# A hybrid network of convolution, scan, attention and experts: its first stage rebuilt

## The reference

```python
out = relu(group_norm(conv(x, w1)))                 # 256 -> 64 channels
om = conv(out, w_off, pad=1) + b_off                # 27 maps: 9 x, 9 y, 9 masks
mask = sigmoid(om[:, 18:])
py, px = grid_y + ky + om[:, 9:18], grid_x + kx + om[:, :9]
sampled = bilinear_sample(out, py, px) * mask       # 9 taps a pixel
out = einsum('bckhw,ock->bohw', sampled, w2)
out = relu(group_norm(out))
x1 = relu(group_norm(conv(out, w3)) + x)            # 64 -> 256 channels
h = group_norm(x1)
# pixel order of each of two heads, from four numbers a, b, c, d
w = (a * z + b) / (c * z + d + 1e-6)                # z: complex point of a pixel
perm = argsort(real(w) + 1.3 * imag(w))
```

## Time and profile before

| | |
|---|---|
| time of the whole program, median of 3 runs | 942.29 us (939.59 to 943.25) |
| profiled execution, first to last instruction (span) | 936.3 us |
| TensorE busy | 764.8 us, 82% of the span |
| VectorE busy | 594.6 us, 64% |
| ScalarE busy | 483.4 us, 52% |
| POOL busy | 298.5 us, 32% |

### The profile page before, as it was taken

How to read it: one execution, slowest core, us unless ns; L and a number is a source line. 1 busy time by engine, 2 the same in 40 slices (tenths; PEclk the granted TensorE clock), 3 DMA queues, 4 the chain that set the end, 5 groups by cost and what they waited for, 6 DMA issues and landing times. The chain is left out here.

```text
span 936.3 us, 17800 instructions
## 1 busy us (share of the span) xinstructions
PE 764.8 (82%) x6400; PEld 431.4 (46%) x6400; DVE 594.6 (64%) x1303; ACT 483.4 (52%) x618; POOL 298.5 (32%) x246
## 2 busy tenths in 40 slices
PE   3959638999988798649999667787659999999993
PEld 1848426633664465533444244454534444444442
DVE  4985343399777674466667376564576777677763
ACT  4134134643134556237778324445337877778871
POOL 1061000077220100034555220334024444566640
PEclk8579857999989999769999979889879999999996
DMA  3000036000023430431111243792523156522114
GB/s 119 1 0 1 0 121 295 1 0 1 1 66 100 131 94 4 140 112 35 46 47 41 67 128 99 229 250 79 174 84 105 49 184 239 187 69 70 64 57 147
DMA packets 55197, 85.21 MB, mean 91 GB/s; under 512 B 10532, under 2 KB 46500, under 8 KB 51908
## 3 DMA queue, kind: packets, MB, share of 16 engines
q1 hardware_dynamic: 48040, 67.42, 22.5%
q0 software_dynamic: 7072, 16.66, 5.4%
HBM read 59.01 MB, written 12.32 MB: 76 GB/s over the span
## 5 line engine op out<-in xcount | busy, mean ns | idle before, releaser
L2162 PE MATMUL psum<-ring,f_x_t 128*32 x432 | 197.1, 599 | 2.4 <-DVE f_x_t L1970 2.4
L2166 PE MATMUL psum<-f_w_up,f_x_t 128*32 128x512 f32 x864 | 197.4, 599 | 0.0
L1976 DVE COPY f_w_up<-ring 128x2048 f32 x108 | 131.5, 1219 | 12.8 <-issue 12.1
L2064 ACT ACTIVATE f_w_down<-ring 128x1024 f32 x108 | 108.2, 1056 | 0.0
L2187 PE MATMUL psum<-ring,f_gated_t 128*32 x432 | 102.1, 379 | 1.7 <-issue 1.7
L2191 PE MATMUL psum<-f_w_down,f_gated_t 128*32 128x256 f32 x1296 | 102.8, 379 | 0.0
L2166 PE MATMUL psum<-h,f_x_t 128*32 128x512 f32 x216 | 99.3, 603 | 0.0
L2166 PE MATMUL psum<-x,f_x_t 128*32 128x512 f32 x216 | 97.8, 595 | 0.0
L2162 PEld LDWEIGHTS psum<-ring,f_x_t 128*32 128x32 f32 x432 | 43.3, 110 | 109.9 <-issue 109.9
L1859 POOL DMA_INDIRECT rows_out<-f_y,f_to_row x36 | 64.6, 1795 | 89.6 <-DVE f_y L1992 51.2
L1850 POOL DMA_INDIRECT f_xs<-rows_in,f_from_row x54 | 74.8, 1386 | 40.1 <-PE psum L2150 20.7
(11 more groups left out here) (298 smaller groups left out, 1674.9 us busy)
## 6 DMA issues: line engine op xcount, KB each, us to landing
ring<-in_f_experts SPq DMA_DIRECT2D x24, 1536.0 KB, 7.6
a_stack_q<-a_parts SPq DMA_DIRECT2D x96, 64.0 KB, 2.0
a_stack_k<-a_parts SPq DMA_DIRECT2D x96, 64.0 KB, 2.0
rows_in<-h SPq DMA_DIRECT2D x4, 1024.0 KB, 12.1
ring<-rows_out SPq DMA_DIRECT2D x8, 512.0 KB, 5.5
earlier_y<-f_y POOLq DMA_DIRECT2D x18, 128.0 KB, 2.9
f_earlier_y<-earlier_y POOLq DMA_DIRECT2D x18, 128.0 KB, 3.2
ring<-in_a_wqkv SPq DMA_DIRECT2D x2, 768.0 KB, 4.4
```

The source lines that it names most:

```text
L1976: dve.tensor_copy(w_up[tile, q % 2], k.ring[:, bass.ds(at[tile - 1], 2 * CT * CHUNK)]).then_inc(s_uv, 1)
L2064: act.activation(w_down[:, tile - 1, q % 2, :], k.ring[:, bass.ds(at[tile - 2] + 2 * CT * CHUNK, CHUNK // P * C)], ACT.Copy).then_inc(s_da, 1)
L2162: pe.matmul(psum[0:QUARTER, 2 * b + side, :], x_t[:, b, t, 0:QUARTER], k.ring[:, bass.ds(at + start, CHUNK)], start=first, stop=final, til ...
L2166: last = pe.matmul(psum[rows, 2 * b + side, :], x_t[:, b, t, rows], w_up[tile, b][:, start:start + CHUNK], start=first, stop=final, tile_p ...
```

## The change

All of it is in the first stage and in the arrays prepared for it.

- Loads: x in two halves, each with a semaphore; the identity, the norm's tensors and w_off under semaphores of their own. ScalarE's queue loads `mobius` and `z`; `z` holds only a partition's own two pixels. TensorE starts with three products on w1.
- Scores: `scores` computes only the partition's own two pixels for both heads, 25 steps of up to 8 elements, ahead of the first statistics. `spread` turns them on TensorE, so that every partition has all 256 in PSUM. `rank` is eight VectorE steps and a reduction, behind the image; POOL makes the one-hot rows.
- Image: one padded image on all 128 partitions, without shifted copies: two images by ScalarE, two by VectorE in two steps each. POOL makes an unpadded copy, `plain`.
- Offsets: w_off is the stationary operand, 32 columns on tiles of 64 rows x 32 columns; the lower 64 partitions have taps 0 to 4, the upper ones taps 5 to 8, in two banks, and one column tile belongs to one image. ScalarE and VectorE add the two, TensorE turns the sum.
- Weights: six pieces of two images and three taps; all outer products on VectorE, four of 768 elements a piece, all evictions of turns on ScalarE. `mix` runs as two 64-row halves; VectorE takes four of the eight.
- Sampling: 18 steps, each with the turns of one tap of two images, then the sampling of the tap before.
- Tail: statistics straight from PSUM, eight and four identity products around the second group mean, the second norm's result by ScalarE and VectorE, the third convolution on 64-row halves, image pair by image pair.

The core of the diff:

```diff
@@ PixelOrder
+    def spread(self, pe, bank, ident):
+        pe.wait_ge(self.s_value, 1)
+        for h in range(HEADS):
+            for t in range(NT):
+                last = pe.transpose(bank[:, N * h + P * t:N * h + P * t + P],
+                                    self.value[:, h, t:t + 1].broadcast_to([P, P]), ident)
+        last.then_inc(self.s_spread, 1)
...
+                dve.scalar_tensor_tensor(self.tie[:, NT * h + t, :], scores, self.value[:, h, t:t + 1], self.before[:, t, :],
                                          ALU.is_equal, ALU.mult).then_inc(self.s_rank, 1)
...
+                dve.scalar_tensor_tensor(self.less[:, i, :], scores, self.value[:, h, t:t + 1], self.tie[:, i, :],
+                                         ALU.is_lt, ALU.add).then_inc(self.s_rank, 1)
...
+        dve.tensor_reduce(self.rank_of[:].rearrange("p h t -> p (h t)"), self.less[:], AX_X, ALU.add).then_inc(self.s_rank, 1)
@@ gpsimd
-                pool.tensor_tensor(weights[:, b % 2, 1, :, :].rearrange("p k (y x) -> p k y x", y=HW),
...
+            pool.wait_ge(s_img, B)
             for b in range(B):
+                pool.tensor_copy(plain[:, b].rearrange("p (y x) -> p y x", y=HW),
+                                 image[:, b, 1:HW + 1, 1:HW + 1]).then_inc(s_plain, 1)
+            order.one_hot(pool)
@@ vector
+            order.scores(dve)
...
+            for i, b in enumerate((2, 3)):
+                inner = image[:, b, 1:HW + 1, 1:HW + 1]
+                dve.tensor_scalar(inner, psum[:, y_banks + 1, N * i:N * i + N].rearrange("p (y x) -> p y x", y=HW),
+                                  g1.scale[:, b:b + 1], g1.shift[:, b:b + 1], ALU.mult, ALU.add).then_inc(s_scaled, 1)
+                dve.wait_ge(s_scaled, i + 1)
+                dve.tensor_scalar(inner, inner, 0.0, None, ALU.max).then_inc(s_img, 1)
+            order.rank(dve, psum[:, SCORE_BANK, :])
...
+            def sampling(q):
+                dve.wait_ge(s_hat, q + 1)
+                if q >= 2:
+                    dve.wait_ge(s_tr, PAIR_LOADS * (q - 1))
+                for half in range(2):
+                    for t in range(NT):
+                        T = NT * half + t
+                        dve.tensor_tensor(weights[:, q % 2, half, t].rearrange("p k (y x) -> p k y x", y=HW),
+                                          hat[:, q, T, KT:, :].unsqueeze(3).broadcast_to([P, KT, HW, HW]),
+                                          hat[:, q, T, :KT, :].unsqueeze(2).broadcast_to([P, KT, HW, HW]),
+                                          ALU.mult).then_inc(s_wd, 1)
...
+            distances(0)
+            distances(1)
+            take_mixed(1)
             mask_hats(0)
             sampling(0)
+            distances(2)
             mask_hats(1)
+            sampling(1)
+            take_mixed(4)
+            distances(3)
+            mask_hats(2)
+            sampling(2)
+            take_mixed(5)
...
@@ scalar
+            for q in range(PIECES):
+                for j in range(PAIR_LOADS):
+                    J = PAIR_LOADS * q + j
+                    b, tap = 2 * (q // THIRDS) + j % 2, KT * (q % THIRDS) + j // 2
+                    act.wait_ge(s_tr, J + 1)
+                    act.activation(weights_t[:, b, tap].rearrange("p s n -> p (s n)"), psum[:, J % 4, :], ACT.Copy).then_inc(s_ev, 1)
+                    if j == 1 and q + 2 < PIECES:
+                        tents(q + 2)
+                    if q == 2 and j == PAIR_LOADS - 1:
+                        take_mixed(7)
@@ tensor
+            for n in range(FIRST_TAPS):
+                for j in range(B):
+                    pe_rows = slice(QUARTER * j, QUARTER * j + QUARTER)
+                    for channels, tap, bank in ((lower, n, OM_BANKS[0]), (upper, FIRST_TAPS + n, OM_BANKS[1])):
+                        if tap >= TAPS:
+                            continue
+                        final = tap in (FIRST_TAPS - 1, TAPS - 1)
+                        last = pe.matmul(psum[pe_rows, bank, 0:N], w_off[channels, n, :],
+                                         image[channels, j, tap // 3:tap // 3 + HW, tap % 3:tap % 3 + HW],
+                                         start=(n == 0), stop=final,
+                                         tile_position=(channels.start, QUARTER * j))
...
+            for u in range(PIECES * KT):
+                for half in range(2):
+                    turn(u // KT, 2 * (u % KT) + half)
+                if u:
+                    sample(u - 1)
+                if u in MIX_AFTER:
+                    i = MIX_AFTER[u]
+                    if i == 4:
+                        pe.wait_ge(s_moa, 2)
+                    else:
+                        pe.wait_ge(s_mod, i - 3)
+                    mix(i)
+            sample(PIECES * KT - 1)
+            square_identity(pe, k, psum[:, SPARE_BANK, :], 4)
+            g2.group_mean(pe, psum[:, 4, 0:2 * PAIRS], pair[:])
+            square_identity(pe, k, psum[:, SPARE_BANK, :], 8)
```

More of the change, by code:

```diff
@@ L189, in products @@
[L189 to L213, removed]
@@ L447, in _ @@
         def _(act):
+            order.load_points(act, k)
             order.root(act)
@@ L476, in _ @@
[L476 to L484 removed]
+            take_mixed(0)
@@ L506, in _ @@
             pe.wait_ge(s_w1, 16)
-            pe.wait_ge(s_x, 16)
+            for _ in range(3):
+                pe.matmul(psum[:, SPARE_BANK, 0:P], w1[:, 0, :], w1[:, 0, :], start=True, stop=True)
             for half in range(2):
+                pe.wait_ge(s_x[half], 16)
                 for t in range(CT):
@@ L549, in sample @@
+            def sample(u):
+                i, tap = u // TAPS, u % TAPS
+                if u == 0:
+                    pe.wait_ge(s_moa, 3)
+                    pe.wait_ge(s_mod, 1)
+                if u == TAPS:
+                    pe.wait_ge(s_moa, 4)
+                    pe.wait_ge(s_mod, 4)
+                pe.wait_ge(s_ev, 2 * (u + 1))
+                for s in range(NT):
                     for half in range(2):
@@ L575, in _ @@
-            sample(1)
-            g2.group_mean(pe, psum[:, 4, 0:B], pair[:])
-            pe.wait_ge(s_r2, B // 2)
-            for t in range(CT):
-                for b in range(B):
-                    last = pe.matmul(psum[:, 2 * t + b // 2, (b % 2) * N:(b % 2) * N + N], w3[:, b % 2, P * t:P * t + P],
-                                     r2[:, b // 2, :], start=True, stop=True)
-                    if b % 2:
-                        last.then_inc(s_c3, 1)
+                                         mixed[:, b, s, tap, :], weights_t[:, b, tap, s, :],
@@ new lines, in sample @@
+                                         start=(tap == 0 and s == 0), stop=(tap == TAPS - 1 and s == NT - 1))
+                if tap == TAPS - 1:
+                    last.then_inc(s_y, 1)
+            pe.wait_ge(s_w, LOADED)
+            mix(0)
+            pe.wait_ge(s_omc, 1)
+            turned = psum[:, OM_T_BANK, 0:TT * QUARTER].rearrange("p (b s o) -> p b s o", b=B, s=NT)
+            for s in range(NT):
+                last = pe.transpose(turned[:, :, s, :], om_c[:, P * s:P * s + P], k.ident_sb[:])
@@ new lines, in _ @@
+            last.then_inc(s_omt, 1)
+            mix(1)
+            pe.wait_ge(s_moa, 1)
+            mix(2)
+            pe.wait_ge(s_mod, 1)
+            mix(3)
+            pe.wait_ge(order.s_rank, order.READ)
+            pe.wait_ge(s_mask, 1)
+            for u in range(PIECES * KT):
+                for half in range(2):
+                    turn(u // KT, 2 * (u % KT) + half)
[8 more added lines that the diff above has]
+                    mix(i)
```

498 lines of the change are left out of this document (259 added, 239 removed).

## The result

Four runs of the changed kernel have a median of 901.14 us (898.85 to 906.88), four of the kernel before, beside them, 942.77 (939.59 to 943.69): ratio 0.9561, 95% interval 0.9515 to 0.9607. The forecast was 903, between 890 and 921. The profiled execution took 901.77 us, its span is 900.0.

The account below looks back on a forecast made before the run. The limit changes by stretch (DMA, norm chain, TensorE, outer products, serial tail). First stage 67.1 + 8.1 + 15.6 = 90.8 against 129.7, 38.9 less; 936.3 - 38.9 = 897.4, plus 6.0 gives 903 us, range 890 to 921.

Parts of the forecast that it names:

- row halves do not overlap: Rival: offsets' row halves run one after another, taking 15.5 us, mixes 1.0 more; 915 us in all; chance 0.10.
- VectorE paces the loop: Rival: a three-tap product costs 2.0 us, 24 take 48, loop ends near 79; 916 us in all; chance 0.06.
- TensorE stays at its lower level: Rival: TensorE at 1.2 GHz through the stage, loop 77.2 us for 38.6; 948, up to 970; low clock chance 0.06.
- The change gives little: Rival: front and tail already paced by DMA and omitted chains; 921 us in all; chance 0.04.
- part 5: Loop of turns, sampling and mixes, 49.2 us before: 18 steps of 1.97, mixes 3.5, 39.0 in all; last sample at 67.1.
- Part 1: Loads and scores, up to 15.95 us before: 2.5 us earlier, bounds 0 and 4; norm ready at 13.5.
- Part 2: Image, 5.85 us before: ScalarE and VectorE write side by side, shifted copies go; 1.4 us, ready at 14.9.
- Part 3: Offsets, 20.68 us before: 72 records in 3.9 us, VectorE's ranks 5.1 end last at 20.0; positions at 21.3.
- Part 4: Positions to first turn: distance steps, eviction, mask and four products take 5.4 us; first image pair complete at 26.7.
- The clock's charge of 1.8: Loop start: 4 us of work at half pace, as TensorE pauses ahead of the loop; 1.8 us net.
- Part 6: Tail, last sample to last statistic: 8.1 us against 11.7, or 11 with the clock low; the 15.6 behind stays.
- The 6.0 us that I added: Whole kernel: median of shown runs lies 6.0 us above the profiled span, added to the predicted span of 897.4.

Follow-up runs that it names:

- sixth experiment: Changed kernel with the offset product running all taps of the lower 64 rows first, then all of the upper; 905.06 us, 0.962 of the kernel before.
- eleventh experiment: Changed kernel with six warming products, groups of three taps, later ranks' reduction and six identity squares ahead of mix 3; 895.31 us, 0.9491 of the kernel before.
- fifth experiment: Changed kernel with sampling in groups of three taps, one piece behind the turns, and the last mix one step later; 900.44 us, 0.9556 of the kernel before.
- tenth experiment: Changed kernel with nine identity products added in TensorE's pauses between offsets and loop; 902.87 us, 0.955 of the kernel before.
- third: Changed kernel with all nine taps of two images turned first, then nine samplings in one block; 909.21 us, 0.9634 of the kernel before.
- seventh experiment: Changed kernel without the eight and four identity products around the second group mean; 906.43 us, 0.9609 of the kernel before.

## Why the prediction was right, and which terms were off

Each step of the sum, from the end of the one ahead of it, in us:

```
step                                predicted  measured  difference
loads and norm, to the image           13.5      16.2      +2.7
image                                   1.4       1.8      +0.4
image to positions                      6.4       5.4      -1.0
positions to first pair's products      5.4       6.0      +0.6
products to last sample                40.4      41.4      +1.0
last sample to last statistic           8.1       7.9      -0.2
to stage two                           15.6      15.7      +0.1
stage two at                           90.8      94.4      +3.6
```

**The mechanism held.** The image, the offsets, the loop and the tail shrank where the prediction put it, and TensorE became the bound of the loop, as its 41.37 busy of 41.40 us show. Against *row halves do not overlap*: 72 records in 2.39 us, where one after another they were put at 15.5. My 3.9 (four at once) was too high: eight start within 0.05 us of each other, and such groups follow 0.215 apart. A mix has its turns start 0.69 behind its own start (36.54 to 37.23), nearer to the overlapped end than my 0.9. Against *VectorE paces the loop*: 24 products have a mean of 0.958 us, and VectorE is busy 23.52 of 41.40. Against *TensorE stays at its lower level*: the granted clock is 1.00 from 36 us on. *The change gives little* was priced at 921, and the time is 901. One of the prediction's own signs of being wrong did appear, a granted clock of 0.50 past 32 us: it lasted until about 35 and is priced under part 5.

**Part 1 failed.** I took 2.5 us off the norm; nothing came off (16.16 here, 15.98 in the earlier trace rows). x in halves starts the convolution 0.4 earlier (5.96 for 6.35), but its eight records take 6.34 us, 5.25 before: most of the first six start 0.85 apart, and from 11.2 us on they follow at about half of that. The granted-clock column reads 1.00 throughout this stretch, but the trace's entries on the clock begin only at 11.31, and in all 13 profiles the first entry (7.56 to 11.85 us) stands in the record in which the pace doubles; before it the column shows no measurement. That ties the pace to the granted clock. What stands ahead of the convolution moves that rise, but does not settle it: with six products and no pause the eight records take 4.52 to 5.26 us (three profiles), with three and a pause 5.16 to 6.56 (eight), with none, in the kernel before, 5.25 and 5.05. So the three products that the change put there did not bring the rise forward; why it came later still in five of these eight profiles stays open.

**Part 2** took 1.8 us for 1.4: VectorE's two steps an image are 0.84 and not 0.7.

**Part 3** was mis-sized twice, and only one mattered. The offsets took 2.39 and not 3.9, which changes nothing, as they do not end last (sixth experiment); the ranks, which end last, took 4.5 us (17.73 to 22.21) and not 5.1. The eleventh experiment, with their reduction of 1.22 moved, has the positions 1.15 sooner behind the image.

**Part 4**: two distance steps took 1.18 for the 0.86 of the sum, the mask 0.36 for 0.25, the four products 3.72 for 3.6. The price of an element, read from a step of 2304, was too low for the small steps.

**Part 5**: a step is 2.04, not 1.97, since a change between turns and samples costs 0.15 (fifth experiment), not 0.11; 18 of them are 1.3 more. The mixes gave 0.8 back (four at 0.69 for 0.9). The clock's charge of 1.8 lies between the 1.2 and 2.7 of the tenth experiment, and this trace had the upper. The Trainium skill, "TensorEngine Tiling (Array Packing)", Key Properties, says that a change of mode drains the engine. The trace agrees, at 0.15 for each change, and the third and fifth experiments show that an order which saves changes gains only when the other queues keep moving. The Trainium skill, "TensorE: Matmul & The Clock Gate", Part 4, says that transposes do not bring the full clock. Here the measurement decides otherwise: the loop, half turns, ran at 1.00.

**Part 6** came out at 7.85 for 8.1, with errors that cancel: the statistics start 1.21 us behind the third convolution, not 0.7, and the eight take 2.75, not 3.4. The squares that I named as its cover were worth 0.03 (seventh experiment): VectorE's statistics set the end. The 11 that I put for a low clock is not tested in full, since without the squares the clock fell only during the third convolution.

**That the number came so close is in part luck.** The first stage is 3.6 longer than predicted and the rest 1.0 shorter, so the span is 897.4 + 3.6 - 1.0 = 900.0; what I added around it was 4.2 too much, which hides the 3.6. The 6.0 us that I added are 1.8 here (901.77 - 900.0), and in the second trace of the kernel before 937.36 - 935.6, again 1.8. The 6.0 was no constant: 936.3 and 935.6, with 1.8 added, lie below the medians of the timed runs (942.77 and 941.37), so these two executions were quick ones. So the medians differ by 41.6 us and the stages of the profiled runs by 35.3 (129.7 to 94.4) to 36.5 (129.48 to 92.97); the other 5 or 6 us lie in the scatter of the unchanged rest, and whether part of them belongs to the change stays open.

## What to carry to other kernels

Price a stage on the path of its own stretches and in its own trace; compare its end, not the whole time, where the untouched rest scatters by more than the edit. When one engine must alternate two tile forms, count the changes, at 0.15 us each here, but group only as far as the queues of the other engines still run. Where the clock column shows no change at the start of an execution, go by the pace of the records. Work that fills a pause ahead of a long matmul stretch is worth what the low clock costs there, about 1 to 3 us here, and nothing where another engine sets the end.

## What was not expected of the hardware

Eight 64x32 tiles ran side by side: 72 records of 256 columns in 2.39 us, as eight groups of eight and two of four (the halves have five and four taps), 0.215 apart; with the two row halves issued apart it was 3.28. Products on VectorE and POOL at the same time slowed VectorE from 0.89 (3.57 over 4) to 1.57 (3.13 over 2) each, so that the two finished later (POOL's two in 4.44) than VectorE alone (four in 3.57). And the same program left its low clock at different times, near 35 us in one execution and near 32 in the next, which alone moves the stage by 1.5 us.
